# Graph attention and eight-head attention on one core: four score banks, one bank for transpositions, halves in place of pairs, and another order of the work

## What is computed

```python
# x: 32 graphs of 512 nodes x 512; adj: 512 x 512 mask with about 3% ones
# layer 0
h = x @ W                                   # 512 -> 256
e = leaky_relu(h @ a[0] + (h @ a[1]).T, 0.2) + NEG * (1 - adj)
g = concat(softmax(e) @ h, h)
x = layernorm(x + g)
# layer 1
q, k, v = heads(x @ Wq.T + bq), heads(x @ Wk.T + bk), heads(x @ Wv.T + bv)   # 8 heads of 64
s = where(adj == 0, -inf, q @ k.T / 8)
x = layernorm(x + merge(softmax(s) @ v) @ Wo.T + bo)
```

## Time and profile before

| | us |
|---|---|
| median of 3 runs | 3236.22 (3234.52 to 3239.79) |
| the profiled execution, on the device | 3235.14 |
| its span, first to last instruction | 3233.3 |
| TensorE busy in it | 3015.4 |
| from the third N's matmuls (184.01) to the thirtieth's (2824.71), 27 rounds | 2640.7, so 97.8 a round |

### The profile page before, as it was taken

One profiled execution on the slowest core, in us unless ns is written; L12 is line 12 of the kernel. 1 busy time (PEld: TensorE's weight loads), 2 busy tenths in 40 slices (PEclk: granted clock), 3 DMA queues, 4 the chain that ended last, 5 costly groups with the idle time before them and its releaser, 6 DMA issues.

```text
span 3233.3 us, 60175 instructions
## 1 busy us (share of the span) xinstructions
PE 3015.4 (93%) x19084; PEld 2496.1 (77%) x19084; DVE 2604.6 (81%) x6553; ACT 2427.2 (75%) x5383; POOL 2070.5 (64%) x1799
## 2 busy tenths in 40 slices
PE   5899999999999999999999999999999999999995
PEld 4787788777787787787777787777887777887874
DVE  4888888888888888888888888888888888888873
ACT  4777777777777777877777877777877778777764
POOL 1566676666666666766666666666666666766664
PEclk8999999999999999999999999999999999999997
DMA  3777777777777777787777777777777777777774
GB/s 124 201 207 213 223 214 226 208 209 215 217 222 221 207 212 214 222 230 213 208 210 222 221 224 212 210 210 217 222 224 208 205 214 222 220 227 206 212 203 143
DMA packets 290044, 681.90 MB, mean 211 GB/s; under 512 B 40512, under 2 KB 74048, under 8 KB 256960
## 3 DMA queue, kind: packets, MB, share of 16 engines
q1 hardware_dynamic: 289728, 678.05, 73.8%
HBM read 375.40 MB, written 302.51 MB: 210 GB/s over the span
## 4 chain that ended last, share of the span: by engine, by line
PE 49%; DMA 25%; POOL 10%; SPq 5%; ACT 5%; issue 3%; DVE 3%; ACTq 0%; DVEq 0%; POOLq 0%
PE R_bank L621 30%; DMA turned_lo_prob<-scratch 17%; PE O_bank L708 9%; POOL turned_lo_prob L1054 8%; DMA scratch<-blocked 8%; PE S_bank L689 6%; SPq L523 4%; PE L_bank L612 2%; ACT turned_hi_prob L736 2%; DVE blocked L995 1%; SPq L540 1%; POOL turned L1074 1%; PE L_bank L621 1%; POOL o_pair L1049 1%; DVE prob L975 1%
## 5 line engine op out<-in xcount | busy, mean ns | idle before, releaser
L1054 POOL TENSOR_TENSOR turned_lo_prob<-turned_lo_prob,turned_hi_prob 128x512 fp32r<-128x512 f32 x1024 | 1312.0, 1312 | 671.5 <-ACT turned_hi_prob L736 671.5
L995 DVE STREAM_TRANSPOSE blocked<-prob 128x512 f32<-128x512 f32 x1024 | 695.4, 699 | 185.9 <-ACT prob L817 127.9
L736 ACT ACTIVATE turned_hi_prob<-turned_lo_prob 128x512 fp32r<-128x512 f32 x1024 | 593.5, 622 | 329.1 <-DMA turned_lo_prob<-scratch 322.8
L817 ACT ACTIVATE prob<-prob,negmax 128x512 f32<-128x512 f32 x1024 | 730.3, 714 | 89.2 <-DVE negmax L975 88.1
L975 DVE CUSTOM_DVE_ANT_0 prob<-S_bank,mask 128x512 f32<-128x512 f32 x1024 | 681.1, 679 | 83.5 <-PE S_bank L689 77.1
L689 PE MATMUL S_bank<-qk_pair 64*128 64x512 f32 x3072 | 495.3, 427 | 84.9 <-DVE negmax L975 83.5
L708 PE MATMUL O_bank<-turned_hi_prob,v_st 128*128 128x256 f32 x2048 | 517.6, 290 | 48.9 <-POOL turned_lo_prob L1054 48.5
L708 PE MATMUL O_bank<-turned_lo_prob,v_st 128*128 128x256 f32 x2048 | 508.4, 285 | 0.0
L708 PEld LDWEIGHTS O_bank<-turned_hi_prob,v_st 128*128 128x128 f32 x2048 | 396.6, 194 | 73.2 <-POOL turned_lo_prob L1054 67.9
L621 PE MATMUL R_bank<-wv,x1T 128*128 128x256 f32 x3072 | 415.4, 288 | 0.2 <-DVE v_st L874 0.2
L621 PEld LDWEIGHTS R_bank<-wv,x1T 128*128 128x128 f32 x3072 | 381.7, 191 | 38.3 <-issue 35.5
(11 more groups left out here) (75 smaller groups left out, 4315.6 us busy)
## 6 DMA issues: line engine op xcount, KB each, us to landing
scratch<-blocked SPq DMA_DIRECT2D x256, 1024.0 KB, 4.6
turned_lo_prob<-scratch SPq DMA_DIRECT2D x1024, 256.0 KB, 5.6
tokens<-xT SPq DMA_DIRECT2D x128, 256.0 KB, 5.0
tokens<-x SPq DMA_DIRECT2D x128, 256.0 KB, 4.8
r_wide<-r_scratch SPq DMA_DIRECT2D x512, 64.0 KB, 3.6
out<-tokens SPq DMA_DIRECT2D x128, 256.0 KB, 4.0
r_scratch<-r_cols SPq DMA_DIRECT2D x256, 2.0 KB
tokens<-adj SPq DMA_DIRECT2D x1, 1024.0 KB, 7.6
```

Source lines behind the costliest of these rows:

```text
L736: act.activation(dst, src, ACT.Copy).then_inc(done, 1)
L817: act.activation(prob_tile(R, s), prob_tile(R, s), ACT.Exp, bias=negmax[:, slot:slot + 1], scale=-1.0, accum_out=psum_row[:, ph % 2, j:j + ...
L995: dve.transpose(blocked[:, ph % 2, :, :, 2 * (s % 2) + s % 4 // 2, :].rearrange("p d c i -> p c d i"), prob_tile(R, s).rearrange("p (c d i ...
L1054: pool.tensor_tensor(turned_lo_prob[:, ph % 2, a, :, :], turned_lo_prob[:, ph % 2, a, :, :].bitcast(F32), turned_hi_prob[:, a, :, :].bitca ...
```

## The change

- Four S_banks, tile s in bank s mod 4; unit u now waits until both tiles of unit u-2 are reduced. The matmuls of `scores` are issued as before, two tiles together.
- One L_bank for B, N, C and E. Each waits until all before it is emptied.
- N is copied by ACT to a new tile `n_wide` in SBUF, and `pre` reads that. C0 waits for the copy.
- `o_pair` becomes `o_half`: ACT and POOL split each half by itself (`turn`, eight of 128x256 in place of four of 128x512). `lows` of each half waits for the split of the half before.
- All five lists, START, PROLOGUE and ENDING are new. Rounds start at scores unit 4 instead of 3.
- Small columns share tiles; `stats` has two slots in place of four. No instruction changes by that.

```diff
 TENSOR_PLAN = (
-    "scores k1 N",
-    "weigh weigh scores",
-    "C0 scores O0",
-    "O1 scores C1",
-    "O2 weigh weigh",
-    "O3 scores q2",
-    "k2 D0 weigh",
-    "weigh D1 W0",
-    "scores C2 W1",
-    "scores W2 W3",
-    "scores C3 D2",
-    "weigh weigh scores",
-    "D3 q3 k3",
-    "weigh weigh E0",
-    "E1 scores scores",
-    "V0 A3 V1",
-    "scores E2 E3",
-    "weigh weigh scores",
-    "B0 q4 k4",
-    "weigh weigh B1",
-    "scores V2 scores",
-    "B2 V3 q1",
-    "weigh weigh scores",
-    "B3",
+    "k1 N weigh",
+    "weigh scores scores",
+    "O0 O1 O2",
+    "C0 scores scores",
+    "weigh weigh O3",
+    "q2 k2 C1",
+    "weigh D0 weigh",
+    "scores scores A3",
+    "D1 W0 W1",
+    "C2 W2 W3",
+    "weigh C3 D2",
+    "weigh scores scores",
+    "D3 q3 k3",
+    "weigh weigh E0",
+    "scores scores E1",
+    "scores E2 V0",
+    "V1 E3 weigh",
+    "weigh B0 scores",
+    "q4 k4 weigh",
+    "weigh B1 V2",
+    "scores scores V3",
+    "scores B2 weigh",
+    "weigh q1 B3",
+    "scores",
 )
...
 SCALAR_PLAN = (
-    "evQ1 pre0 exp lows",
-    "aexp0 exp pair pre1",
-    "exp exp hi C0",
-    "hi hi hi aexp1",
-    "exp pre2 exp exp",
-    "exp lows hi hi",
-    "hi hi evQ2 exp",
-    "C1 aexp2 exp lows",
-    "fin0 hi evW0 fin1",
-    "pre3 hi hi evW1",
-    "exp C2 hi aexp3",
-    "evW2 pair evW3 exp",
-    "exp exp C3 fin2",
-    "fin3 hi hi exp",
-    "hi lows hi exp",
-    "exp A0 exp evQ3",
-    "lap0 lap1 lows E0",
-    "E1 hi hi hi",
-    "hi exp exp evV0",
-    "lap2 lap3 exp E2",
-    "E3 exp pair exp",
-    "hi hi hi evV1",
-    "B0 hi A1 lows",
-    "exp exp evQ4 exp",
-    "lows A2 hi hi",
-    "evV2 hi exp A3",
-    "hi exp evV3 B1",
-    "exp exp B2 pair",
-    "hi hi lows B3",
-    "hi exp hi exp",
+    "evQ1 exp exp lows",
+    "N turn pre0 hi",
+    "exp hi aexp0 hi",
+    "hi exp exp pre1",
+    "exp C0 exp hi",
+    "hi hi hi aexp1",
+    "lows exp exp evQ2",
+    "pre2 exp turn aexp2",
+    "C1 fin0 hi exp",
+    "hi hi evW0 hi",
+    "fin1 evW1 lows pre3",
+    "C2 evW2 exp aexp3",
+    "evW3 fin2 exp exp",
+    "C3 turn fin3 hi",
+    "exp hi hi hi",
+    "lows A0 exp exp",
+    "exp evQ3 lap0 lap1",
+    "turn E0 lap2 hi",
+    "E1 hi hi exp",
+    "lows hi E2 lap3",
+    "exp exp E3 exp",
+    "turn evV0 evV1 hi",
+    "lows hi hi exp",
+    "hi A1 B0 exp",
+    "exp evQ4 exp turn",
+    "A2 hi hi hi",
+    "B1 lows hi exp",
+    "evV2 exp evV3 exp",
+    "B2 A3 turn exp",
+    "lows hi hi hi",
+    "B3 hi exp exp",
+    "turn",
 )
...
 VECTOR_PLAN = (
-    "vt reduce reduce vt",
-    "evQ1 red0 sum reduce",
-    "vt vt reduce inv",
-    "red1 vt vt C0",
-    "reduce evO0 reduce vt",
-    "evO1 yst0 yst1 reduce",
-    "evO2 reduce vt vt",
-    "vt inv red2 evO3",
-    "yst2 reduce sum reduce",
-    "yst3 evQ2 evD0 yrs",
-    "C1 vt vt lst0",
-    "sum evD1 inv reduce",
-    "reduce evW0 red3 reduce",
-    "evW1 vt C2 lst1",
-    "evW2 reduce evW3 vt",
-    "vt evD2 reduce C3",
-    "vt reduce reduce lst2",
-    "evD3 vt sum lst3",
-    "reduce lrs inv vt",
-    "vt evQ3 vt sum",
-    "E0 reduce reduce reduce",
-    "E1 vt vt evV0",
-    "reduce inv reduce E2",
-    "E3 vt vt vt",
-    "inv reduce evV1 reduce",
-    "reduce sum vt vt",
-    "evQ4 vt sum B0",
-    "reduce inv reduce reduce",
-    "vt evV2 reduce vt",
-    "vt B1 B2 evV3",
-    "vt inv reduce reduce",
-    "sum B3",
+    "vt reduce vt reduce",
+    "evQ1 sum vt vt",
+    "reduce inv red0 reduce",
+    "evO0 vt reduce reduce",
+    "yst0 vt vt evO1",
+    "evO2 reduce reduce red1",
+    "yst1 vt vt yst2",
+    "inv evO3 C0 reduce",
+    "reduce sum yst3 yrs",
+    "vt evQ2 red2 evD0",
+    "vt C1 vt reduce",
+    "lst0 reduce evD1 reduce",
+    "vt evW0 reduce evW1",
+    "sum red3 evW2 C2",
+    "lst1 vt evW3 inv",
+    "vt C3 vt reduce",
+    "evD2 reduce vt reduce",
+    "evD3 reduce lst2 lst3",
+    "lrs sum vt vt",
+    "evQ3 vt E0 reduce",
+    "reduce inv E1 reduce",
+    "vt reduce E2 sum",
+    "vt vt E3 vt",
+    "evV0 evV1 inv reduce",
+    "reduce vt sum reduce",
+    "reduce vt B0 vt",
+    "vt evQ4 inv reduce",
+    "reduce B1 sum reduce",
+    "evV2 evV3 vt vt",
+    "reduce B2 inv sum",
+    "vt vt reduce inv",
+    "reduce B3",
 )
...
 GPSIMD_PLAN = (
...
+    "norm turn",
+    "lo lo",
+    "lo lo",
+    "lo lo",
+    "lo lo",
+    "norm yrs",
+    "lo lo",
+    "turn lo",
+    "lo norm",
+    "turn lo",
+    "lo lo",
+    "lo lrs",
+    "norm turn",
+    "lo lo",
+    "lo lo",
+    "A0 norm",
+    "bo0 bo1",
+    "turn lo",
+    "lo lo",
+    "lo A1",
+    "norm turn",
+    "A2 lo",
+    "lo lo",
+    "lo norm",
+    "turn A3",
+    "norm lo",
+    "lo lo",
+    "lo bo2",
+    "turn bo3",
 )
...
 SP_PLAN = (
...
+    "mv sv",
+    "rl mv",
+    "rs sv",
+    "mv sv",
+    "rs fin0",
+    "rl fin1",
+    "mv xt0",
+    "fin2 xt1",
+    "sv rs",
+    "rl mv",
+    "sv fin3",
+    "rs rl",
+    "mv sv",
+    "rl xt2",
+    "ld0 rs",
+    "mv ld1",
+    "sv xt3",
+    "rl ld2",
+    "rs mv",
+    "rl rs",
+    "ld3 sv",
+    "rs rl",
 )
...
-START = "A0 A1 A2 B0 B1 w0 A3 w1 B2 B3"
+START = "A0 A1 B0 w0 A2 B1 w1 A3 B2 B3"
...
-PROLOGUE = """pre0 red0 ld0 w2 aexp0 N C0 D0 red1 pre1 red2 aexp1 pre2 C1 evD0 D1 w3 aexp2 C2 red3 pre3 aexp3 D2 evD1
-              evD2 lst0 C3 lst1 lst2 evD3 lst3 lrs ld1 ld2 D3 bb lap0 lap1 lap2 lap3 ld3 E0 E1 E2 A0 E3 evV0 bw evV1
-              evQ4 reduce reduce bo0 A1 vt vt V0 exp exp V1 bo1 q4 k4 A2 sv B0 scores evV2 V2 reduce reduce vt exp B1
-              exp scores V3 bo2 bo3 reduce A3 vt evV3 B2 reduce scores q1 exp exp inv B3 rs"""
...
+PROLOGUE = """ld0 red0 ld1 w2 N pre0 aexp0 C0 red1 evD0 pre1 aexp1 D0 pre2 red2 C1 w3 D1 aexp2 C2 pre3 red3 aexp3 D2
+              lst0 evD1 ld2 evD2 lst1 C3 D3 sv bb lst2 evD3 lst3 A0 lrs lap0 lap1 bw E0 E1 lap2 bo0 bo1 lap3 V0 ld3
+              bo2 evV0 E2 V1 evV1 E3 evQ4 reduce q4 reduce k4 V2 B0 scores scores A1 reduce vt reduce exp exp evV2
+              evV3 exp rs exp vt vt vt A2 V3 B1 reduce reduce exp A3 scores q1 inv B2 B3 scores bo3 exp"""
...
-ENDING = """norm sum weigh weigh evO0 evO1 yst0 lows yst1 evO2 O0 O1 O2 yst2 evO3 O3 pair fin0 fin1 fin2 yst3 fin3
+ENDING = """sum norm evO0 weigh lows weigh turn fin0 fin1 fin2 fin3 evO1 yst0 evO2 O0 O1 yst1 yst2 O2 O3 evO3 yst3
...
-SAME_BANK = {"B0": 1, "B1": 3, "C0": 1, "C1": 1, "C2": 1}
-SECOND_BANK = {"B1", "B3", "C0", "C1", "C2", "E0", "E2"}
...
-        o_pair = sb("o_pair", [P, N])
+        o_half = sb("o_half", [P, 2 * P])
+        n_wide = sb("n_wide", [P, N])
...
-        S_bank = [bank(f"S_bank{i}") for i in range(3)]
...
+        S_bank = [bank(f"S_bank{i}") for i in range(4)]
         O_bank = bank("O_bank")
         R_bank = [bank(f"R_bank{i}") for i in range(2)]
-        L_bank = [bank(f"L_bank{i}") for i in range(2)]
+        L_bank = bank("L_bank")
...
-            return L_bank[name in SECOND_BANK]
+            return L_bank
...
-            return S_bank[(32 * R.k + s) % 3]
+            return S_bank[s % 4]
...
             def solo(R, name):
-                before = solo_count(R, name, 1 - SAME_BANK.get(name, 2))
+                before = solo_count(R, name, 0)
...
                 if kind == "N":
                     pe.wait_ge(terms_ready, R.nx(4, 4))
-                    pe.wait_ge(solo_done, R.nx(len(SOLO), 3))
+                    pe.wait_ge(solo_done, R.nx(len(SOLO), 4))
                     for j in range(T):
-                        last = pe.transpose(L_bank[0][:, j * P:(j + 1) * P], terms[:, j, 1:2].to_broadcast([P, P]),
+                        last = pe.transpose(L_bank[:, j * P:(j + 1) * P], terms[:, j, 1:2].to_broadcast([P, P]),
                                             ident[:, :])
                     last.then_inc(n_mm, 1)
                 if kind == "C":
                     pe.wait_ge(a_exp, R.nx(4, i + 1))
+                    if i == 0:
+                        pe.wait_ge(n_copied, R.nx(1, 1))
                     if i == T - 1:
                         pe.wait_ge(a_pre, R.nx(4, T))
                     solo_turn(solo(R, name), alpha[:, :])
...
                 if kind == "O":
                     out_b = ring(R, name)
                     if i == 0:
-                        pe.wait_ge(o_lo, R.n(4, -1))
+                        pe.wait_ge(o_lo, R.n(8, -2))
                     project(out_b[:, :], lambda s, c: oT[:, s, c, i * P:(i + 1) * P],
-                            lambda m, c: wo[:, m, c, :], ring_mm, R.n(4, 0) if i == 0 else None)
+                            lambda m, c: wo[:, m, c, :], ring_mm, R.n(8, 0) if i == 0 else None)
 
             def scores(R, u):
                 pair, t = u // T, u % T
-                if R.prologue and t == 0:
+                if R.prologue and u == 16:
                     pe.wait_ge(w_lo, 5)
                     pe.wait_ge(bias_done, 1)
                 if t == 0:
                     pe.wait_ge(ring_done, R.ring(f"k{pair}", 1))
-                if due(R.n(32, 2 * u - 1)):
```

(23 more changed lines are left out.)

92 lines of the change are left out of this document (25 added, 67 removed).

## The result

Before: 3235.37 us (median of 4 runs, 3233.50 to 3239.79). After: 3201.51 us (median of 4 runs, 3193.84 to 3203.22). The ratio is 0.9882, with a 95% interval of 0.9863 to 0.9901: faster by 1.2%. The forecast of 3192 lies 9.5 us under the median.

A forecast was written before the change was run, and what follows sets the result against it. TensorE was taken as the bound, busy 93.4 of a 97.8 us round. Idle time falling from 4.42 to 2.95 gives 1.47 x 30 = 44 us less, 1 more for the ends: 3235.1 to 3192, range 3130 to 3245.

The forecast's parts named there:

- The floor: TensorE's work in a steady round: 93.4 us, unchanged by the edit, so only 4.45 us of idle time can go.
- Four banks: TensorE's waits before score units and C0: those of unit 6 and C0 go, 1.22 in the E stretch becomes 0.8.
- One L_bank: E stretch: single bank shared by transposed tiles; with unit 14's 0.8 the stretch costs 2.0 us a round.
- E2: Third E tile on TensorE, in the E stretch: held 0.2 us until E1's low part empties the L_bank.
- E3: Last E tile on TensorE, in the E stretch: held 0.5 us until the low part of the tile before is done.
- Rival (c): Slower by the single L_bank at its E and B tiles: mean drain 3.1 gives 3269 us; chance 0.15.
- Probabilities: Weigh passes, from a phase's last scores to its weigh: waits of 0.8 us a round become 0.6.
- Rival (b): The stall moves to the weighs, mainly weigh 14 and weigh 0: no change, 3235 us; chance 0.14.
- Copies and halves: N's copy and split halves: ScalarE 75.5 to 76.6 us a round, GpSimd 64.7 to 65.5; O0 waits 0.1.
- Start and end: START's shared bank costs nothing, prologue +2 us, the last half's split -1; bounds +10 and -8.
- The sum: Whole run: idle time 2.95 us a round in place of 4.42, 44 us less, 1 more for the ends: 3192.

The follow-up runs named there:

- apart: Kernel after with adjacent score units on TensorE taken apart by other work, four pairs in effect: 3262.88 us, ratio 1.0069.
- three_banks: Kernel after with three score banks in place of four, one L_bank, the eighth bank empty: 3515.93 us, ratio 1.0855.
- e1_first: Kernel after with one name moved: ScalarE takes E1's high part before the first hi of phase 4: 3194.78 us, ratio 0.9868.
- old_order: Lists of the kernel before on the banks and waits of the kernel after, with only forced moves: 3738.32 us, ratio 1.1539.
- after_third: Kernel after, unchanged, measured a third time beside later edits: 3198.10 us, ratio 0.9884.
- e_no_vt: Kernel after with parts of E1, E2 and E3 moved ahead on ScalarE and VectorE, vt 23 left behind evQ3: 3194.36 us, ratio 0.9872.
- start_x: Kernel after with SyncE loading the first tile of x before it waits for the mask: 3197.96 us, ratio 0.9879.
- after_again: Kernel after, unchanged, measured once more beside other edits: 3202.63 us, ratio 0.9888.
- three_two: Kernel after with three score banks and two L_banks, which B, C and E take in turn: 3517.21 us, ratio 1.0863.

## Why the prediction was right, and where not

**The floor** was wrong. "The edit changes no matmul. So 93.4 is the floor": the busy time is 92.56. The list was priced by the distance of each name from the next, in the surroundings of the old list, and side by side two score units cost less, as `apart` shows. With the groups that grew set against it, the busy time fell by 0.81 a round, nearly half of the 1.74.

**Four banks** was right, and even cautious. The waits before unit 6 and unit 13 went, unit 14's stayed, at 0.46 in place of the 0.8 that I gave it (12.3 us in 27 rounds, forecast 22). three_banks shows that the list could not have been written without the fourth bank.

**One L_bank** had the right sum for the wrong reason. The stretch was to cost 2.0 and cost 2.0 (unit 14 0.46, E2 1.24, E3 0.28); that the parts add up to the forecast is luck. I had put 0.2 on E2, and 0.5 each on E3 and on B0, which waits for nothing; the E tiles' waits are 41 us in 27 rounds, with about 30 forecast. The step that failed is "E1's low part comes behind two reductions and an inversion": I walked VectorE's list and not ScalarE's, where E1's high part stood behind a transfer. e1_first shows this. Rival (c) was rightly kept: with the old lists its mechanism costs 10.8 us a round. The Trainium skill (Perfetto Trace Analysis, Matmuls) says that independent groups of matmuls should rotate through PSUM banks. The runs agree at both ends: three_banks pays 10.9 us a round for its missing score bank, old_order 10.8 for its single L_bank. The kernel after pays 1.5 for the same single bank, because its list puts other work between the users of that bank.

**Probabilities** were undersized: 0.6 a round forecast for the weighs, 29.1 / 27 = 1.08 in this profile and 33.7 / 27 = 1.25 in after_third. Weigh 12 was 0.49 as forecast (0.4); weigh 14 was 0.53, forecast 0.2. It is this term that makes idle time 3.54 a round and not 2.95. Rival (b) is the one that the experiments bring out: not for this change, but for what comes next. e_no_vt took 36.5 us from the E tiles and paid 27.5 at the weighs.

**Copies and halves**: ScalarE is busy 2462.9 us, 35.7 more, as forecast (35). GpSimd is 4 us less busy, not 25 more: the split of the halves cost 24.2 more (189.9 against 165.7), as forecast, but the 1024 low parts of the probabilities cost 14 less (1312.0 before, 1297.7 after) and the additions of bo_wide 11 less, in another order of the same work. The wait for alpha went (22.2 to 1.3), as forecast from C0's new place. What the halves and the copy do by themselves was not tried.

**Start and end**: "START's Bs share a bank while the weight transfers are under way: nothing" was wrong by 3.0 us at B1 (22.21 against 19.21), shown by start_x. In all the start cost 8.4 us at the third N, inside the bounds of +10 and -8, where I took +2. Of it 4.5 us are there at the first N (36.54 against 32.02), before any score unit or E tile, where the prediction had put nothing; start_x takes back 1.6 of them. Another 3.5 come up to the second N (100.84 against 92.81). The score unit more that I gave as a reason is none: six units stand ahead of the second N in both kernels. What the E drains have in it was not separated. The end gave 1.8, forecast 1.

**The sum**: the forecast gain was 43 us, 44 from 1.47 a round in 30 rounds less 1 for the ends. In the profiled execution it was 41.2: 47.8 from 1.65 a round in 29, less 8.4 and plus 1.8. So the number came out near because two misses, the cheaper score pairs (0.8 a round too little) and the weighs with the start (0.5 a round and 6 us too much), lean against each other. That is luck. The medians' gain is 34, 9.5 us short of the forecast. The traces of after_again and after_third have rounds of 96.4 and 96.3 in place of 96.1, so 1.4 to 1.6 under the kernel before, which is nearer to what this kernel does in most of its executions.

## What to carry to other kernels

When a bank is given to one use and taken from another, the order of the work decides whether that helps: walk each engine's list from the matmul to the bank's last reader, and look for any wait for a transfer that stands in it. Price a list of matmuls by its neighbours as well as by its names. And before a stall is removed, measure the slack of the chain that is next; here it was 0.8 us before the first weigh after E3, and the rest of the gain stopped there.

## What the runs showed of the hardware

- After a wait of 3.19 us TensorE's granted clock was 0.54 for the next 3.66 us of work. Shorter waits did not always do this: in three_banks the clock was 1.00 in the 3.7 us after a wait of 2.47, but 0.54 after one of 2.02 that had a wait of 1.12 some 1.6 us of work ahead of it. In old_order one of 2.46 (before C0, at 1583.33) was followed by 3.67 us at 0.50. Below, the stretches of three_banks after its 2.02 and its 2.47:

```profile
1646.23:1649.90 3.67, 3.67 (x17) 2.94 (x18) 1.93 (x4) 2.89 (x7) 3.50 (x4) 0.54 0.83 203
1691.93:1695.60 3.67, 3.67 (x18) 2.76 (x19) 1.55 (x6) 1.83 (x5) 1.26 (x2) 1.00 0.95 340
```

- Two score units in a row cost 1.58 us from start to start of what follows (a pair by itself: 0.80 and 0.78), a lone one 0.89. Each pair taken apart cost 0.28 us of busy time in the score matmuls' group.
- The 512-wide matmuls of q and k take longer in all the changed kernels: 237 ns from start to start on average, against 231 (k) and 233 (q) before. Their groups are busy 647.6 us in 27 rounds against 636.3, some 0.4 us a round. Their operands and their number are the same. three_two, with the banks of before, and old_order, with the lists of before, show it too, so neither the banks nor the order by itself is the cause. What these two still share with the kernel after, N's copy, the halves and the new places of tiles in SBUF, was not tried; the cause stays open. Without it the change would have won about 12 us more.
